# Heads' squares by pairs of chunks, gate projections inside the scan, and gating ahead of the chunk matrices in a gated linear-attention block

## What is computed

```python
x = hidden_states                                   # [8, 256, 256]
q = causal_dwconv_silu(x @ Wq.T, conv_wq)           # heads of 32; k the same, v with heads of 64
beta = sigmoid(x @ Wb.T); g = -exp(A_log) * softplus(x @ Wa.T + dt_bias)
q = l2norm(q) * DK ** -0.5;  k = l2norm(k)
def step(S, inp):                                   # over the 256 tokens
    S = S * exp(gt)
    S = S + bt * kt (vt - kt S)^T
    return S, qt S
o = o * rsqrt(mean(o * o, -1) + eps) * norm_w
o = (o * silu(x @ Wg.T)) @ Wo.T
x = layernorm(x + o)
x = layernorm(x + ternary(x) @ (ternary(weight) + rram_variation).T)
```

## Time and profile before

| | |
|---|---|
| median of 3 runs | 410.98 us (410.93 to 413.01) |
| the profiled execution | 416.89 us |
| its span, first to last instruction | 415.1 us |
| PE busy | 262.5 us (63%) |
| DVE busy | 283.4 us (68%) |
| ACT busy | 138.2 us (33%) |
| mean granted clock of TensorE | 0.799 of full speed |

### The profile page before, as it was taken

How to read it: one execution, slowest core, us unless ns; L and a number is a source line. 1 busy time by engine, 2 the same in 40 slices (tenths; PEclk the granted TensorE clock), 3 DMA queues, 4 the chain that set the end, 5 groups by cost and what they waited for, 6 DMA issues and landing times.

```text
span 415.1 us, 15255 instructions
## 1 busy us (share of the span) xinstructions
PE 262.5 (63%) x6994; PEld 187.3 (45%) x6994; DVE 283.4 (68%) x718; ACT 138.2 (33%) x269; POOL 8.5 (2%) x14
## 2 busy tenths in 40 slices
PE   2992744687590948785753678677906187694742
PEld 1391612475450725565522445666505166554521
DVE  0574899868859586678389677688496852208996
ACT  0684422255361143343730322543800202135010
POOL 2000100010000000010000000100000000000000
PEclk9975778599897769699895968996957565898665
DMA  7600000000000010000010100000100001001001
GB/s 250 245 0 2 3 0 2 3 5 5 6 2 0 10 42 3 3 6 6 17 38 0 51 2 5 3 5 3 55 0 1 0 3 54 5 4 54 2 0 51
DMA packets 8016, 9.78 MB, mean 24 GB/s; under 512 B 1808, under 2 KB 7056, under 8 KB 7952
## 3 DMA queue, kind: packets, MB, share of 16 engines
q1 hardware_dynamic: 7024, 8.41, 5.9%
q10 hardware_dynamic: 928, 0.39, 0.4%
HBM read 6.70 MB, written 2.10 MB: 21 GB/s over the span
## 4 chain that ended last, share of the span: by engine, by line
PE 46%; DVE 28%; issue 15%; ACT 8%; DMA 2%; DVEq 0%; SPq 0%; ACTq 0%
PE pj L340 11%; PE fr L329 9%; PE pg L329 5%; PE pc L329 4%; PE pc L484 3%; PE po L329 3%; PE fr L507 3%; PE fr L593 2%; PE po L484 2%; DVE r_all L895 2%; DVE t_all L894 2%; DVE t_all L893 2%; DMA xt<-x_t 2%; PE pj L354 2%; DVE o_ch L1082 2%
## 5 line engine op out<-in xcount | busy, mean ns | idle before, releaser
L340 PE MATMUL pj<-xt,wproj 128*128 128x512 f32 x96 | 57.8, 749 | 14.0 <-DMA xt<-x_t 8.2
L915 DVE SCALAR_TENSOR_TENSOR conv_buf<-raw,wconv,conv_buf 128x512 f32<-128x512 f32 x72 | 53.1, 750 | 17.3 <-ACT conv_buf L642 15.6
L641 ACT ACTIVATE raw<-pj 128x512 f32<-128x512 f32 x24 | 14.3, 598 | 79.9 <-PE pj L340 79.7
L340 PEld LDWEIGHTS pj<-xt,wproj 128*128 128x128 f32 x96 | 21.4, 237 | 37.0 <-issue 27.6
L484 PE MATMUL pc<-wout,o_ch 128*128 128x256 f32 x36 | 14.0, 566 | 34.0 <-DVE o_ch L1082 34.0
L484 PEld LDWEIGHTS pc<-wout,o_ch 128*128 128x128 f32 x36 | 10.5, 301 | 38.8 <-DVE o_ch L1082 36.4
L1046 DVE TENSOR_TENSOR mq<-fr,ad 128x512 f32<-128x512 f32 x12 | 8.3, 688 | 19.8 <-PE fr L329 19.8
L329 PE MATMUL pg<-x,p_sb 32*32 32x16 f32 x768 | 10.6, 196 | 12.4 <-issue 11.7
L1056 DVE TENSOR_REDUCE m_o<-x_buf 128x24 f32<-128x1536 f32 x3 | 5.3, 1753 | 18.6 <-ACT x_buf L731 18.6
L329 PE MATMUL fr<-kga,wu 32*32 32x64 f32 x768 | 12.7, 215 | 7.8 <-issue 7.8
L495 PE MATMUL pg<-identb,tok_buf 128*128 128x128 bf16 x24 | 3.1, 311 | 21.2 <-DVE tok_buf L1122 21.2
(11 more groups left out here) (181 smaller groups left out, 610.4 us busy)
## 6 DMA issues: line engine op xcount, KB each, us to landing
xt<-x_t SPq DMA_DIRECT2D x1, 1536.0 KB, 10.9
res<-x SPq DMA_DIRECT2D x3, 512.0 KB, 3.9
out<-hid_buf SPq DMA_DIRECT2D x6, 256.0 KB, 2.9
wproj<-w_proj SPq DMA_DIRECT2D x1, 1024.0 KB, 9.0
xt<-x_t SPq DMA_DIRECT2D x1, 512.0 KB, 6.9
kq<-x SPq DMA_DIRECT2D x1, 512.0 KB, 3.9
out<-wu SPq DMA_DIRECT2D x2, 256.0 KB, 2.1
wout<-w_out SPq DMA_DIRECT2D x1, 384.0 KB, 10.5
```

Source lines behind the costliest of these rows:

```text
L340: mm = pe.matmul(pj[:, j % 2, :], wproj[:, t, j * P:(j + 1) * P], xt[:, t, k * TOK:(k + 1) * TOK], start=(t == 0), stop=(t == KT - 1))
L641: act.activation(raw[:, SLOT[j], :, TAPS - 1:], bank, ACT.Copy)
L915: e = dve.scalar_tensor_tensor(out=conv[:, d, :, :], in0=raw[:, d, :, m:m + T], scalar=wconv[:, j, m:m + 1], in1=conv[:, d, :, :], op0=ALU ...
```

## The change

1. The squares of the heads are taken by ACT for two chunks at a time, right behind the copy of these two chunks (`heads_square`), into a buffer of their own, `o_sq`, in all four turns. `o_square` and `end_square` go.
2. The gate projections of the front turns move into the scan, at the end of its steps 4, 5 and 6, into the two banks of `pj`; ACT's `gate_silu` stands at the same steps. In turn 3 they stay on PE, and ACT's silus stand one step earlier. `exponents` now waits for the silus, since it writes `pj`.
3. On PE `project(k+2, 0)` and `(k+2, 1)` move ahead of `project_out`, `project(k+2, 2)` ahead of the transposes, and `project(k+2, 3)` behind `merge(k+1)`. ACT's copies follow; that of tile 3 goes to the start of the next turn.
4. On DVE `gated(k)` moves ahead of `chunk_matrices(k+1)`.
5. On ACT the silus of the value tiles 4 and 5 stand one step of the scan earlier.

```diff
-        o_sq = view(x1_buf, 0, U, DV)
+        o_sq = sb("o_sq", [P, G3, NC, DV])
...
-                bank = (pg, pc, po)[j] if not last(k) else pj[:, j % 2, :]
-                if not last(k):
-                    after(pe, s_done, NC - 1, k, NC - 1)
-                    after(pe, o_out, 3, k, NC // 2)
-                elif j == 2:
+                if j < 2 and not last(k):
+                    after(pe, tile_out, CONV_TILES, k + 1, CONV_TILES)
+                if j == 2:
                     after(pe, gate_done, 1, k, GATE_TILES)
...
+                if not first(k):
+                    after(pe, gate_done, 0, k, GATE_TILES)
...
+            def heads_square(k, n):
+                after(act, o_out, n + 1, k, NC // 2)
+                if n == 0 and not first(k):
+                    after(act, on_scaled, 0, k, 1)
+                act.activation(o_sq[:, :, 2 * n:2 * n + 2, :], o_all[:, :, 2 * n:2 * n + 2, :],
+                               ACT.Square).then_inc(osq_done, 1)
...
+                if front and not first(k):
+                    tile_out_of_psum(k + 1, 3)
...
                     if c % 2:
                         heads_out(k, c // 2)
+                        heads_square(k, c // 2)
...
-                after(dve, osq_done, 1, k, 1)
+                after(dve, osq_done, NC // 2, k, NC // 2)
...
                 head_norm(k)
+                gated(k)
                 chunk_matrices(k + 1)
-                gated(k)
```

68 lines of the change are left out of this document (22 added, 46 removed).

## The result

| | before | changed |
|---|---|---|
| median | 412.0 us | 389.32 us (387.13 to 392.11) |
| ratio, 95% interval | | 0.944, 0.936 to 0.952 |
| profiled execution, its span | 416.89, 415.1 us | 392.11, 390.3 us |
| PE, DVE, ACT busy | 262.5, 283.4, 138.2 us | 258.9, 282.9, 139.7 us |
| mean granted clock | 0.799 | 0.829 |

The medians differ by 22.7 us (forecast 24.8 off 410.98, a time of 386.2). The spans of the two profiled executions differ by 24.8 us, the very sum that was forecast, but that is luck: these two executions lie 4.9 and 2.8 us above the medians of their kernels. No engine does noticeably less; what went is waiting.

What follows compares the result with a forecast made beforehand. No engine bounds throughout; late hand-overs within turns do. Squares and gates 11.6, gating and projections 0 and 1 10.5, projections 2 and 3 0, the end 2.7: 24.8 us off 410.98, giving 386.2 us, range 380.5 to 397.

Runs made afterwards that it cites:

- filler: 28 matmuls of 128x512 in bfloat16 added to the changed kernel in each front turn, in TensorE's idle stretch ahead of the transposes: ratio 0.957, 395.4 us.

## What to carry to other kernels

Where small matmuls come with regular holes, look at which piece a long matmul would stand in before moving it there: the same three gate projections were free in the first steps of the scan and cost 2.1 to 2.6 us a turn in the later ones (0.6 us with another order of projections ahead of the scan). A squaring or copy that waits behind unrelated work of its engine is the cheapest thing to move; here it was most of the gain. In a stretch of small matmuls count the instructions as well as the work: a front scan before the change has 1204 matmuls and weight loads, 4.7 packets of 256, packets came 3.8 us apart, and the scans took 16.2 to 17.5 us for 10 to 12.5 us of work.

## What the runs showed of the hardware

- The instruction queue's packets match the pieces between holes: three times 128 added matmuls with their weight loads gave three packets more (55 to 58). A piece takes 3.9 to 4.0 us even if its work takes 1.99. In 124 of the 133 holes of TensorE in the scans of all profiles, work starts again 1.20 to 1.57 us after such a packet has ended.
- Small matmuls of 8 columns that all use the same 32x32 tile of the array took 47 ns each at a granted clock of 0.62, those of 64 columns spread over four row groups 15.5 ns each at 1.00.
- Stretches alike to the eye, 6 us of filler and 2.3 us of idle time, kept TensorE at the 2.4 GHz level in turn 0 and let it fall to 1.2 GHz in turn 1, with 2.79 and 5.30 us for the same products (5.01 in turn 2, at 0.54 of the clock). Whether such a stretch keeps its clock can't be planned from these traces.
